# Layer normalisation work moved between VectorE and GpSimd in the first attention of an eight-layer kernel

## The reference, cut to what matters

```python
x = x + _L0_xattn_ref(_layernorm(x), ctx_1024, Wq, Wkv, Wo)   # 16 heads of 8, 64 context rows
x = x + _L0_ffn_ref(_layernorm(x), norm_g, norm_b, slot_g, slot_b, scale, slot_embeds, Wg, bg, Wu, bu, Wd, bd)
```

## Time and profile before

| what | value |
|---|---|
| runs | 909.98, 914.59, 913.65 us; median 913.65 us |
| the profiled execution's own time | 909.98 us, with a span of 908.3 us |
| PE, DVE, ACT, POOL busy | 96%, 76%, 59%, 66% of the span |
| mean granted TensorE clock | 0.987 |

### The profile page before, as it was taken

How to read it: one execution, slowest core, us unless ns; L and a number is a source line. 1 busy time by engine, 2 the same in 40 slices (tenths; PEclk the granted TensorE clock), 3 DMA queues, 4 the chain that set the end, 5 groups by cost and what they waited for, 6 DMA issues and landing times.

```text
span 908.3 us, 16088 instructions
## 1 busy us (share of the span) xinstructions
PE 869.5 (96%) x4762; PEld 669.4 (74%) x4762; DVE 691.3 (76%) x1564; ACT 534.0 (59%) x1024; POOL 598.8 (66%) x614
## 2 busy tenths in 40 slices
PE   7998999999999899999999999999999998998997
PEld 5656676666697756888888888888888666775775
DVE  6997777899557889866666666666668778888886
ACT  3556667666743256666666666666666674445475
POOL 5983544688613155877777777777777777888710
PEclk9999999999999889999999999999999999999998
DMA  7000000322001000200000000000002000000001
GB/s 206 2 2 1 1 1 13 98 76 69 13 1 30 1 10 6 73 27 23 23 23 26 26 20 24 25 26 26 20 24 104 1 1 1 1 1 0 2 13 36
DMA packets 27433, 24.47 MB, mean 27 GB/s; under 512 B 3483, under 2 KB 24179, under 8 KB 27251
## 3 DMA queue, kind: packets, MB, share of 16 engines
q1 hardware_dynamic: 27379, 23.80, 8.8%
HBM read 22.74 MB, written 1.05 MB: 26 GB/s over the span
## 4 chain that ended last, share of the span: by engine, by line
PE 73%; DVE 13%; POOL 6%; ACT 5%; issue 2%; DVEq 0%; ACTq 0%; POOLq 0%
PE psum L2022 68%; POOL hh L765 3%; DVE arena L1931 2%; ACT hh L914 2%; PE psum L2190 2%; DVE arena L1575 1%; DVE arena L1572 1%; DVE stats L1449 1%; ACT arena L976 1%; PE psum L2267 1%; PE psum L2052 1%; PE psum L2083 1%; ACT arena L914 1%; DVE arena L1824 1%; DVE arena L1581 1%
## 5 line engine op out<-in xcount | busy, mean ns | idle before, releaser
L2022 PE MATMUL psum<-xw 128*128 128x512 f32 x1248 | 322.9, 394 | 1.7 <-DVE arena L1824 1.0
L728 POOL TENSOR_TENSOR hh<-arena,hh 128x512 fp32r<-128x512 f32 x176 | 228.2, 1297 | 81.5 <-ACT hh L914 80.2
L2022 PEld LDWEIGHTS psum<-xw 128*128 128x128 f32 x1248 | 232.2, 188 | 54.0 <-issue 3.9
L1831 DVE TENSOR_TENSOR psum<-psum,arena 128x512 f32<-128x512 f32 x176 | 123.1, 699 | 97.7 <-PE psum L2022 91.4
L1168 ACT ACTIVATE arena<-psum 128x512 f32<-128x512 f32 x176 | 105.5, 600 | 120.3 <-PE psum L2022 120.2
L914 ACT ACTIVATE hh<-arena 128x512 fp32r<-128x512 f32 x228 | 142.1, 624 | 38.2 <-DVE arena L1931 35.6
L2022 PE MATMUL psum<-hh,wdn 128*128 128x512 f32 x528 | 148.4, 390 | 0.2 <-POOL hh L728 0.2
L1836 DVE TENSOR_TENSOR arena<-psum,arena 128x512 f32<-128x512 f32 x176 | 121.7, 692 | 7.6 <-DVE psum L1831 1.7
L2022 PEld LDWEIGHTS psum<-hh,wdn 128*128 128x128 f32 x528 | 98.9, 188 | 21.1 <-POOL hh L728 0.4
L2022 PE MATMUL psum<-arena 128*32 128x128 f32 (+6 forms) x992 | 86.2, 304 | 4.7 <-ACT arena L914 3.7
L914 ACT ACTIVATE arena<-psum 128x512 f32<-128x512 f32 (+6 forms) x85 | 57.4, 688 | 43.8 <-PE psum L2022 19.2
(11 more groups left out here) (306 smaller groups left out, 1503.8 us busy)
## 6 DMA issues: line engine op xcount, KB each, us to landing
egu<-in_w SPq DMA_DIRECT2D x44, 128.0 KB, 2.0
egu<-in_egu SPq DMA_DIRECT2D x16, 256.0 KB, 2.6
edn<-in_w SPq DMA_DIRECT2D x44, 64.0 KB, 1.8
edn<-in_edn SPq DMA_DIRECT2D x16, 128.0 KB, 2.0
arena<-in_w SPq DMA_DIRECT2D x1, 1536.0 KB, 7.0
X<-in_x SPq DMA_DIRECT2D x4, 256.0 KB, 4.1
arena<-in_ctxTd SPq DMA_DIRECT2D x2, 512.0 KB, 6.0
arena<-in_conv SPq DMA_DIRECT2D x1, 768.0 KB, 4.1
```

What stands on the lines that cost most here:

```text
L728: pool.tensor_tensor(hh[:, s % 4, 1, :], h1[:, s % 2, :], hh[:, s % 4, 0, :].bitcast(F32), ALU.subtract).then_inc(hh_lo, 1)
L1831: dve.tensor_tensor(bank(2 + k), bank(2 + k), sil[:, k, :], ALU.mult).then_inc(prod_done, 1)
L2022: return pe.matmul(dst, lhsT=lhsT, rhs=rhs, start=start, stop=stop)
```

## The change

1. `STATS_BY_POOL` becomes (0, 2), (0, 3), (1, 0), (1, 1), (1, 2). The three `ln_stats` calls of these groups leave DVE's attention loop, and `token_norm` is called for them on POOL.
2. POOL's order becomes: ln_power of groups 0 and 1, keys 1 to 3, `token_norm(0, 2)`, keys 4, `token_norm(0, 3)`, keys 5, `token_norm(1, 0)`, keys 6 and 7, the norm of the slots, `token_norm(1, 1)`, `token_norm(1, 2)`.
3. The scaling of slot_g and slot_b moves from POOL to DVE (step t = 5), with its own count of `se_n`; PE and ACT wait for `se_n` of 2.
4. At grouped steps ACT does `weight_rows(t-1)` ahead of the exponential of t, as at all other steps.
5. `norm_behind(1, u)` is called in DVE's loop. For L = 1 neither of its conditions is met for any tile, so it issues nothing.

```diff
-        STATS_BY_POOL = ((1, 0), (1, 1))
+        STATS_BY_POOL = ((0, 2), (0, 3), (1, 0), (1, 1), (1, 2))
...
-                    if L == 1:
-                        pool.wait_ge(ln_tp, g + 1)
...
-                    ln_power(0, 0)
-                    ln_power(0, 1)
-                    pool.wait_ge(krep_done, 1)
-                    keys(1)
-                    ln_power(0, 2)
-                    keys(2)
-                    keys(3)
-                    ln_power(0, 3)
-                    for b in range(4, B):
-                        keys(b)
...
-                    def token_norm(g):
+                    def token_norm(L, g):
                         s, half, sq = slice(4 * g, 4 * g + 4), slot_half[:, 0:4, :], slot_sq[:, 0:4, :]
-                        pool.wait_ge(x_done, 4 * g + 4)
+                        if L == 0:
+                            pool.wait_ge(x_in[g], 16)
+                        else:
+                            pool.wait_ge(x_done, 4 * g + 4)
                         sums(half, X[:, s, :])
                         then(pool.tensor_scalar(mv[:, s, 0], half[:, :, 0], 1.0 / D, None, ALU.mult))
-                        pool.wait_ge(ln_tp, g + 1)
+                        if L == 1:
+                            pool.wait_ge(ln_tp, g + 1)
                         then(pool.tensor_tensor(xn[:, s, :], X[:, s, :], wide(mv[:, s, 0:1], 4, D), ALU.subtract))
                         then(pool.tensor_tensor(sq, xn[:, s, :], xn[:, s, :], ALU.mult))
                         sums(half, sq)
-                        then(pool.tensor_scalar(veps[:, s], half[:, :, 0], (1.0 + EPS) / D, EPS * EPS, ALU.mult, ALU.add))
+                        if L == 0:
+                            then(pool.tensor_scalar(veps[:, s], half[:, :, 0], 1.0 / D, EPS, ALU.mult, ALU.add))
+                        else:
+                            then(pool.tensor_scalar(veps[:, s], half[:, :, 0], (1.0 + EPS) / D, EPS * EPS, ALU.mult, ALU.add))
                         pool.tensor_tensor(rstd[:, s], veps[:, s], neghalf[:, s], ALU.pow).then_inc(ln_rstd, 1)
...
+                    ln_power(0, 0)
+                    ln_power(0, 1)
+                    pool.wait_ge(krep_done, 1)
+                    for b in range(1, 4):
+                        keys(b)
+                    token_norm(0, 2)
+                    keys(4)
+                    token_norm(0, 3)
+                    keys(5)
+                    token_norm(1, 0)
+                    keys(6)
+                    keys(7)
+
                     pool.wait_ge(w_slots, 16 * N_SLOTS)
-                    then(pool.tensor_scalar(slot_gs[:, :], cols[:, COL["slot_g"]:COL["slot_g"] + 2], scal[:, 0:1], None, ALU.mult))
...
-                    token_norm(0)
-                    token_norm(1)
+                    token_norm(1, 1)
+                    token_norm(1, 2)
                     continue
                 for g in range(NG):
-                    if L != 1 or g == 2:
+                    if L != 1:
                         ln_power(L, g)
...
-                grouped = t % 4 == 2 and t < NT - 2
-                if 1 <= t <= NT and not grouped:
+                if 1 <= t <= NT:
                     weight_rows(t - 1)
...
-                if grouped:
-                    weight_rows(t - 1)
                 if t == NT:
-                    act.wait_ge(se_n, 1)
+                    act.wait_ge(se_n, 2)
...
-                if t in (0, 2):
-                    ln_stats(0, 2 + t // 2)
+                if t == 5:
+                    dve.wait_ge(w_slots, 16 * N_SLOTS)
+                    dve.tensor_scalar(slot_gs[:, :], cols[:, COL["slot_g"]:COL["slot_g"] + 2], scal[:, 0:1], None, ALU.mult).then_inc(se_n, 1)
...
-                    if t == NT - 1:
-                        ln_stats(1, 2)
+                    norm_behind(1, u)
...
-                    pe.wait_ge(se_n, 1)
+                    pe.wait_ge(se_n, 2)
```

More of the change, by code:

```diff
@@ L837, in token_norm @@
                         sums(half, sq)
-                        then(pool.tensor_scalar(veps[:, s], half[:, :, 0], (1.0 + EPS) / D, EPS * EPS, ALU.mult, ALU.add))
+                        if L == 0:
+                            then(pool.tensor_scalar(veps[:, s], half[:, :, 0], 1.0 / D, EPS, ALU.mult, ALU.add))
+                        else:
+                            then(pool.tensor_scalar(veps[:, s], half[:, :, 0], (1.0 + EPS) / D, EPS * EPS, ALU.mult, ALU.add))
                         pool.tensor_tensor(rstd[:, s], veps[:, s], neghalf[:, s], ALU.pow).then_inc(ln_rstd, 1)
-                        pool.wait_ge(ln_rstd, NG + g + 1)
+                        pool.wait_ge(ln_rstd, NG * L + g + 1)
                         pool.tensor_tensor(xn[:, s, :], xn[:, s, :], wide(rstd[:, s].unsqueeze(2), 4, D), ALU.mult).then_inc(ln_xn, 1)
+                    ln_power(0, 0)
[10 more added lines that the diff above has]
+                    keys(7)
                     pool.wait_ge(w_slots, 16 * N_SLOTS)
-                    then(pool.tensor_scalar(slot_gs[:, :], cols[:, COL["slot_g"]:COL["slot_g"] + 2], scal[:, 0:1], None, ALU.mult))
                     slot_sums(slot_raw)
```

## The result

| | median | runs | profiled execution, span |
|---|---|---|---|
| before | 912.40 us | 4 (909.98 to 914.59) | 909.98, 908.3 |
| changed | 925.12 us | 4 (921.87 to 927.32) | 917.54, 915.8 |
| changed, timed again later | 920.83 us | 4 (918.83 to 926.96) | 926.96, 925.2 |

The ratio to before is 1.0137 with a 95% interval of 1.0089 to 1.0185, and 1.0098 (1.0062 to 1.0134) the second time. The forecast was 923, with a range of 918 to 928.

The account below looks back on a forecast made before the run. DVE and PE were taken to pace the attention, PE the dispatch stage. Profiled 909.98 + 8.55 (POOL late) + 2.05 (low clock) = 920.6, taken to the mean 923.3, told as 923; range 918 to 928.

Parts of the forecast that it names:

- POOL's chain: POOL from `keys(1)` at 14.18 to the end of `token_norm(1, 2)` at 91.65, where PE wants that group at 82.31.
- The delay by it: Start of the dispatch stage: PE waits for POOL's last norm, so `dispatch_T(2)` begins at 96.67, not 88.12, 8.55 us late.
- The clock: PE's restart near 91.7 us after idling: clock low at first, costing 2.05 us, between nothing and 4.9.
- ACT's order: Attention, three grouped steps: copying weights ahead of the exponential costs 0.8 us each, 2.4 in all, hidden behind POOL.
- DVE's relief: Attention: three `ln_stats`, 4.2 us in all, leave DVE; worth at most 0.4 at t = 0, nothing at t = 2 and 15.
- wrong: Closing condition: the forecast fails if L2052 for group (1, 2) stands before 85, or the end distance differs from that at 100 us.
- POOL's idle time: Sign on POOL: no idle time between 14 and 91.7 us.
- The last sign: From 100 us on, both traces run at the same distance of 8.5 to 13 us; wrong if the end distance differs.
- the rival of a hidden POOL: POOL's chain stays hidden and the attention decides: 908.5 us, or 914.7 with ACT's order at its price; chance 8%.
- the held clock: Rival: the clock holds through PE's wait before the dispatch stage; 921.3 us, or 918.5 from the fastest run; chance 17%.
- The long slow clock: Rival: the clock stays low for long after PE's restart in the dispatch stage, + 8.55 + 4.9, 926 us; chance 15%.

Follow-up runs that it names:

- experiment 2: Changed kernel with 22 spare 128x128 matmuls on PE, in its wait ahead of the transposes of group (1, 2); 920.1 us, 1.0064 of before.
- experiment 3: Changed kernel with statistics of group (0, 2) back on DVE and the slots' norm ahead of the token norm of (1, 0); 915.21 us, 1.0036 of before.
- experiment 1: Kernel before with only ACT's new order at the grouped steps; 916.14 us, 1.003 of before.
- experiment 5: Changed kernel with POOL's sums cut from seven adds to two in all token norms and the slots' norm, ACT's new order kept; 912.63 us, 1.0028 of before.
- experiment 6: Changed kernel with POOL's sums cut from seven adds to two and ACT's old order at grouped steps; 911.07 us, 0.9994 of before.
- experiment 4: Changed kernel with ACT's old order at the grouped steps; 923.75 us, 1.0104 of before.
- experiment 7: Kernel before with group (1, 2) alone moved from DVE's statistics to a token norm on POOL; 911.43 us, 1.0007 of before.
- experiment 9: Kernel before with 17 spare 128x128 matmuls on PE around 300 to 315 us; 910.84 us, 0.9984 of before.

## Why the prediction was right

- **POOL's chain.** Predicted from the first key copy to the end of the last norm 77.5 us, measured 91.19 - 13.23 = 77.96, of which 0.55 is the wait for tile 3 that I had as met. A token norm took 10.8 us wherever it stood, also beside an idle DVE: the last two ends lie 90.15 - 79.34 = 10.81 apart. The rule of the Trainium skill on the shared interfaces ("GPSIMD Engine Reference", Key points), by which the last two norms would have been quicker, shows no effect in these lengths. Nearly all of DVE's work beside POOL's norms in the attention reads PSUM, and an instruction with two SBUF inputs wasn't tried.
- **The delay by it.** Predicted 8.55 at the third dispatch transposition, measured 8.16 with the clock held (experiment 2); and the delay goes as soon as POOL is in time (experiment 3).
- **The clock.** Predicted 2.05, measured 1.55 at the same landmark, 1.64 counted from the restart. The direction was read rightly from the launch and from the earlier trace rows; the clock was back by about 94.7 us, 3.4 us behind the restart, so the nearer row was that of 3.3 us (1.65) and not the launch. (The matmuls ahead of that row took 3.88 us by the earlier trace rows, and not 3.7.) The sum of both, 9.7, lies 0.9 under the 10.6 forecast. The advice of the Trainium skill ("TensorE: Matmul & The Clock Gate", Part 1) to leave such a ramp out of a model would have missed the 1.55.
- **ACT's order.** Predicted 2.4, in three steps of 0.8; measured 2.38 (experiment 1, from t = 3 on) and 2.39 (experiments 5 and 6), in three steps of 0.8, hidden behind POOL but for what moves POOL's own start (experiment 4).
- **DVE's relief.** Predicted at most 0.4 at t = 0 and nothing at t = 2 and 15, measured 0.49, all at t = 0 (experiment 6). The attention grew by 3.3 us in the trace and not by 2.0. The rest is the low clock from 16 to 20 us in this trace, 0.93 to 0.98 us by experiments 1 and 7, under which the relief doesn't show.
- **What I had wrong.** PE should have waited about 2 us for group (1, 1); the prediction's own 79.6 and 80.8 make that 1.2. It didn't wait: PE came at 80.4, as POOL had just finished at 80.38, because the attention was longer. And POOL's idle time was not nil. Neither touches the sum. The last sign, by which I would be wrong, did come: the distance, 9.71 at 100 us, is 7.5 at the end, and under the 8.5 to 13 named. It is no sign against the mechanism, since low clock at 294.7 and at 902.9 us in the execution of before takes up the 2.2 us between them; the sign itself was badly chosen, for two single executions differ by more than that. In the rival of a hidden POOL the 914.7 does not follow from its 908.5: with ACT's 2.4 that is 910.9, and 914.7 counts a relief of 0.4 and not of 4.2. Of the rivals, the held clock is refuted by the 0.50 in 88 to 94.6. The long slow clock didn't come at the restart, but a stretch of 17 us did in some executions near 736 us, with a price (7.5 us between two executions) that I had not thought of. POOL hidden is refuted for this kernel; where experiments 3, 5 and 6 make it true (915.21, 912.63 and 911.07 us), there is no gain of 4.2.
- **The total.** 923 against 925.12 and 920.83. The sum was right to a microsecond at 98 us; that it was also right at the end is partly luck, with executions spread over 10 us. The sum holds no term for the stretches of low clock in other stages, and these alone put 9 us between two executions of the changed kernel.

**Open.** Why the stretch near 736 us comes in some executions only. The code there is the same in all kernels. Among the profiles it showed only in kernels with the long wait at 85 to 91 us (two of three). But experiment 5, without that wait, has two runs of 919.5 and 920.0 us with mean clocks of 0.977 and 0.975, beside eight of 910.3 to 916.9, so the wait doesn't seem to be needed for it.

## What to carry to other kernels

Moving work off the busier engine is worth what its next wait leaves of it: three blocks of 1.4 us from DVE, busy for 93% of the stage, bought 0.5 us at full clock and nothing that is seen in the changed kernel's own trace. The engine that receives them has to be added up to its own next deadline, instruction by instruction with the gaps between dependent ones (21 of them make 9.3 us busy into 10.8), and everything in its program behind them counts, down to work of the next stage. When such a deadline is missed, PE's wait has a second price behind it, the low clock at the restart, and filling the wait takes away only that one. And before a difference at a landmark is put down to an edit, the granted clock ahead of the landmark has to be compared: here 0.93 of 3.31 us went with a low clock that kernels without the edit show too.

## What the runs showed of the hardware

- In a wait of 5.95 us without a matmul the clock fell to half, and PE ran at half clock for 3.4 us more behind it; 44 passes of spare matmuls in that wait kept the clock at 1.00.
- Two executions of one kernel differ by 9.4 us (917.54 and 926.96), 7.5 of them by a stretch of 17 us at half clock in a stage that the change doesn't touch.
- From 16 to 20 us the same code ran at a granted clock of 1.00 in one profile (before) and 0.61 in another (experiment 7), and the step at t = 3 came 0.98 us later.
- In the execution with spare matmuls (experiment 9) a stretch of 9.7 us that had half clock before had 1.00. By the landmarks about 1.0 us was gained by it, and the whole changed by -0.16% (interval -0.37 to +0.04), where half of the 9.7 would be 4.85. With the full clock PE was busy for 8.23 of the 9.70 us and no longer for 9.63.
